# A two-layer gated cross-attention kernel: a loop written out, work of GpSimd put in another order, and extra matmuls on zeros in TensorE's waits

## The reference, cut to what matters

```python
x = x + tanh(g_xattn[0]) * L0_xattn(ctx, layernorm(x))   # context and latents as keys, 4 heads of 64
x = x + tanh(g_ffn[0])   * L0_ffn(layernorm(x))          # 256 -> 1024 -> 1024 -> 256, weights of +1 and -1
x = x + tanh(g_xattn[1]) * L1_xattn(layernorm(x), ctx)   # 16 heads of 64, 1024 keys
x = x + tanh(g_ffn[1])   * L1_ffn(layernorm(x))          # 16 experts, 4 of them per token, and one shared

# L0_xattn: q and k are RMS-normed per head; the keys are 1024 of the context (masked) and 512 latents
attn = softmax(where(mask, qn @ kn.T, -max)); out = (attn @ v) @ Wo.T + bo
# L1_xattn
out = softmax(q @ k.T / 8) @ v @ Wo + bo
# L1_ffn
y = sum_e combine[:, e] * (silu(x @ w1[e].T) * (x @ w3[e].T)) @ w2[e].T + shared expert
```

## Time and profile before

| | us |
|---|---|
| median of three runs | 1186.76 |
| lowest and highest | 1183.84, 1190.51 |
| the profiled execution, its own time | 1189.64 |
| its span (first to last instruction) | 1187.8 |
| PE busy | 1082.3 (91%) |
| DVE busy | 837.9 (71%) |
| ACT busy | 700.5 (59%) |
| POOL busy | 354.9 (30%) |
| mean granted TensorE clock | 0.971 of full |

### The profile page before, as it was taken

One profiled execution on the slowest core, in us unless ns is written; L12 is line 12 of the kernel. 1 busy time (PEld: TensorE's weight loads), 2 busy tenths in 40 slices (PEclk: granted clock), 3 DMA queues, 4 the chain that ended last, 5 costly groups with the idle time before them and its releaser, 6 DMA issues. The chain is left out here.

```text
span 1187.8 us, 20470 instructions
## 1 busy us (share of the span) xinstructions
PE 1082.3 (91%) x6952; PEld 947.2 (80%) x6952; DVE 837.9 (71%) x1437; ACT 700.5 (59%) x1273; POOL 354.9 (30%) x372
## 2 busy tenths in 40 slices
PE   1879988998899899999989999999999879999998
PEld 1768877787787778888879798888888768888887
DVE  7687756777514498888879788788889565555555
ACT  3477756775623487787867777787877412222232
POOL 5064415442377402101040203111020213344341
PEclk9899998999999999999999999999999879999999
DMA  4000000002022000000100010000000005343432
GB/s 137 21 1 1 1 5 1 1 1 88 25 57 55 26 1 2 1 1 1 37 3 1 1 37 2 2 1 1 28 1 1 27 5 144 93 124 101 115 109 68
DMA packets 20344, 39.47 MB, mean 33 GB/s; under 512 B 5056, under 2 KB 12352, under 8 KB 19744
## 3 DMA queue, kind: packets, MB, share of 16 engines
q1 hardware_dynamic: 20256, 38.32, 10.9%
HBM read 37.07 MB, written 1.25 MB: 32 GB/s over the span
## 5 line engine op out<-in xcount | busy, mean ns | idle before, releaser
L281 PE MATMUL PS<-R 128*128 128x512 f32 (+2 forms) x2728 | 627.7, 375 | 47.5 <-issue 14.7
L281 PEld LDWEIGHTS PS<-R 128*128 128x128 f32 x2728 | 461.6, 196 | 124.6 <-issue 26.9
L1389 DVE TENSOR_TENSOR R<-PS,R 128x512 fp32r<-128x512 f32 x320 | 205.5, 683 | 37.2 <-ACT R L1107 36.3
L1107 ACT ACTIVATE R<-PS 128x512 fp32r<-128x512 f32 x320 | 175.5, 595 | 83.3 <-PE PS L648 82.6
L1073 ACT ACTIVATE FA<-PS,nmax 128x1024 f32<-128x1024 f32 (+1 forms) x160 | 192.4, 1203 | 41.8 <-DVE nmax L1378 21.8
L661 PE MATMUL PS<-R 128*128 128x256 f32 x1408 | 203.1, 290 | 10.4 <-DVE FB L1397 9.1
L648 PEld LDWEIGHTS PS<-eye,FA 128*128 128x128 f32 x1408 | 163.2, 142 | 43.8 <-DVE R L1389 11.0
L648 PE MATMUL PS<-eye,FA 128*128 128x128 f32 x1408 | 189.5, 279 | 8.9 <-ACT FA L1073 3.5
L661 PEld LDWEIGHTS PS<-R 128*128 128x128 f32 x1408 | 179.1, 190 | 18.3 <-issue 14.5
L1378 DVE TENSOR_REDUCE nmax<-PS 128x1 f32<-128x1024 f32 x128 | 155.8, 1221 | 40.8 <-PE PS L281 29.6
L436 POOL TENSOR_SCALAR R<-R 64x512 fp32r<-64x512 f32 x40 | 25.9, 649 | 327.2 <-ACT R L1222 266.7
(11 more groups left out here) (173 smaller groups left out, 1071.3 us busy)
## 6 DMA issues: line engine op xcount, KB each, us to landing
FB<-comb SPq DMA_DIRECT2D x48, 256.0 KB, 3.8
wst<-we_in SPq DMA_DIRECT2D x26, 384.0 KB, 4.0
wst<-w_in SPq DMA_DIRECT2D x4, 1024.0 KB, 5.0
FB<-k_in SPq DMA_DIRECT2D x16, 128.0 KB, 2.0
wst<-w_in SPq DMA_DIRECT2D x3, 512.0 KB, 5.8
x<-x_in SPq DMA_DIRECT2D x2, 512.0 KB, 5.6
FB<-ctxT_in SPq DMA_DIRECT2D x2, 512.0 KB, 4.7
FB<-ctxT_in SPq DMA_DIRECT2D x4, 256.0 KB, 3.8
```

Of the source, the lines that this page charges most:

```text
L281: last = mm(out, a, b, start=(n == 0), stop=(n == len(passes) - 1), skip_group_check=skip)
L1107: a_(L.pt[0][:, (u // 2) % 2, 4 * g_:4 * g_ + 4, (u % 2) * P:(u % 2) * P + P], L.turn(u, g_).rearrange("p (t n) -> p t n", t=4), ACT.Copy) ...
L1389: inc(v.tensor_tensor(lo, turned, hi.bitcast(F32), ALU.subtract), "p_lo")
```

## The change

1. **Loop.** The `Fori` over the second attention's three turns becomes a Python `for` on PE, ACT, DVE and POOL: the same instructions, once for each turn, with constant counts.
2. **First attention, low halves in order of need.** POOL copies slots 0 and 1 of the queries, makes the low halves 0 to 4, then copies slots 2 and 3, then makes the low halves 5 to 7. PE awaits two copies ahead of the first scores, and all four ahead of unit 8.
3. **First exponential.** ACT awaits three low halves of each engine ahead of the first exponential, and all eight ahead of its first `third` copy.
4. **Zeroing in waits.** The two memsets of `zero_spare_queries(L0, 2)` move ahead of line 474's copy in batch 1, behind a wait for the two output projections of batch 0 (`wo_done` 2).
5. **Matmuls on zeros.** Ten ahead of the feed-forward part's first block (behind a wait for `zeroed`); at the head of the expert stage the two that stood ahead of `gate_up(0)` become eight behind it and eight behind `ln_turn`, and ten are added ahead of `down(1)`. Their results are overwritten or add nothing.

```diff
-        def copy_queries(L, C, count):
+        def copy_queries(L, C, count, slots=range(HG)):
...
-            for slot in range(HG):
+            for slot in slots:
...
             last.then_inc(s["bo_added"], 1)
+            if b == 1:
+                pool.wait_ge(s["bo_added"], 2)
+                pool.wait_ge(s["wo_done"], 2)
+                zero_spare_queries(L0, 2)
 
             pool.wait_ge(s["cx_hi"], 4 * b + 4)
...
-            copy_queries(L0, b, (8 * b + 2, 8 * b + 2))
-            if b == 1:
-                zero_spare_queries(L0, 2)
+            copy_queries(L0, b, (8 * b + 2, 8 * b + 2), range(2))
 
             for i in range(8):
+                if i == 5:
+                    copy_queries(L0, b, (8 * b + 2, 8 * b + 2), range(2, HG))
                 pool.wait_ge(s["qk0_hi"], 8 * b + i + 1)
...
-        with pool.Fori(1, NG1) as i:
+        for i in range(1, NG1):
...
-                pe.wait_ge(s["q_twice"], HG * C + HG)
+                pe.wait_ge(s["q_twice"], HG * C + 2)
...
                 if L.layer == 0 and u + 2 == UNITS // 2:
+                    pe.wait_ge(s["q_twice"], HG * C + HG)
...
+            if j == 0:
+                pe.wait_ge(s["zeroed"], 1)
+                for n in range(5):
+                    for w in range(2):
+                        mm(PS[:, 4 + w, :], zero, LNH[:, 0, 512:1024], start=True, stop=False, skip_group_check=True)
             if m == 0:
                 pe.wait_ge(s["ln_lo"], 2 * NB + 2 * (h + 1))
...
-        with pe.Fori(0, NG1 - 1) as i:
+        for i in range(NG1 - 1):
...
-        zero_banks(4)
-        zero_banks(5)
         gate_up(0, 0, 0, 0)
+        for n in range(4):
+            zero_banks(4)
+            zero_banks(5)
         pe.wait_ge(s["x_att"], 4 + 4 * NG1)
         ln_turn(4 * NB + 2, LN_BANKS[1], late1)
+        for n in range(4):
+            zero_banks(4)
+            zero_banks(5)
         down(0, 0, 0, 0)
...
         gate_up(2, 1, 1, 0)
+        for n in range(5):
+            zero_banks(6)
+            zero_banks(7)
         down(1, 0, 0, 1)
...
                         if g_ == 2:
+                            if u == 0:
+                                act.wait_ge(s["qk0_lo"], 8 * C + 8)
+                                act.wait_ge(s["qk0_lo_pool"], 8 * C + 8)
                             first(act, "p_third", U0 + u - 1)
...
-            act.wait_ge(s["qk0_lo"], 8 * b + 8)
-            act.wait_ge(s["qk0_lo_pool"], 8 * b + 8)
+            act.wait_ge(s["qk0_lo"], 8 * b + 3)
+            act.wait_ge(s["qk0_lo_pool"], 8 * b + 3)
...
-        with act.Fori(0, NG1 - 1) as i:
+        for i in range(NG1 - 1):
...
-        with dve.Fori(0, NG1 - 1) as i:
+        for i in range(NG1 - 1):
```

## The result

| | before | changed |
|---|---|---|
| median of 5 runs, us | 1190.51 | 1176.74 |
| lowest and highest | 1183.84, 1192.71 | 1174.45, 1180.80 |
| the profiled execution: its time, its span | 1189.64, 1187.8 | 1178.63, 1176.5 |

What follows compares the result with a forecast made beforehand. PE, busy 91% of the span, was taken to bound the kernel through idle and lower-clock stretches. Terms summed to -11.15 us: 1178.5 from the profiled 1189.64, 1175.6 from the median 1186.76; forecast 1176, 8-in-10 range 1170 to 1183.

Steps and rivals of the forecast that it cites:

- Loop, -6.3: Second attention: writing the loop out removes two jumps costing 3.28 and 2.99 us; bounds -5 to -7.
- hidden already: Second attention's loop: the register arithmetic for the counts also goes, but was given no gain.
- Batch 0, -1.6: First attention, batch 0: two copies fewer ahead bring the first exponential 1.6 us sooner; bounds 0 to -2.4.
- Batch 1, -3.5: First attention, batch 1: two copies and two memsets fewer ahead bring the exponential 3.5 us sooner; bounds -1.5 to -3.6.
- The +0.7 for a lower clock: First attention, batch 1: lower clock over the transposes after longer PE idle time costs 0.7 us, middle of 0 and 1.5.
- Memsets, +0.65: Gap between batches: memsets delay line 474's copy, and PE with it, by 0.65 us; bounds 0 to +1.
- Zeros ahead of the feed-forward part, +2.6: Feed-forward start: ten matmuls on zeros push the layer norm's root and transposes back, costing 2.6 us; bounds 0 to +5.3.
- Nothing later absorbs it: After the feed-forward zeros: the delay carries on, since the next stage waits for the last of these blocks.
- Head, -3.7: Expert stage's head: zeros fill PE's gaps, keeping full clock over down(0) and the router; saves 3.7 us, bounds -5.3 to +5.8.
- the larger value: Expert head: -5.3 us if gate_up(1) and (2) also run at full clock; not taken.

Runs made afterwards that it cites:

- e1: The kernel before with only the second attention's loop written out on four engines; ratio to before 0.9957, 1185.08 us.
- e10: The changed kernel with PE's loop over the expert tiles written out too; ratio to before 0.9906, 1178.60 us.
- e5: The kernel before with only the low halves in order of need, PE awaiting two copies; ratio to before 1.0000.
- e6: The kernel before with only the first exponential's wait cut to three low halves of each engine; ratio to before 1.0000.
- e6b: The kernel before with the order of need and the shorter exponential wait together, nothing else; ratio to before 0.9982.
- e8: The changed kernel with the feed-forward zeros moved behind block 3 and the two memsets behind line 474's copy; ratio to before 0.9875, 1175.01 us.
- e11: The changed kernel with nine wide matmuls on zeros mixed between the router's groups; ratio to before 0.9909, 1178.67 us.
- e2: The changed kernel without the ten matmuls on zeros ahead of the feed-forward part; ratio to before 0.9883, 1177.45 us.
- e3: The changed kernel with the expert stage's head as before, two matmuls on zeros ahead of gate_up(0); ratio to before 0.9931, 1183.23 us.
- e7: The changed kernel with the ten feed-forward zeros moved from ahead of block 0 to behind block 3; ratio to before 0.9892, 1173.84 us.
- e4: The changed kernel with the two memsets back behind the copies of query slots 0 and 1; ratio to before 0.9924, 1180.84 us.
- e8b: The changed kernel without the feed-forward zeros and with the two memsets behind line 474's copy; ratio to before 0.9894, 1175.46 us.

## Why the prediction was right

The forecast was 1176 with a gain of 11.15 us from the profiled execution; measured were 1176.74 and, between the two profiled executions, 11.0. By its steps:

1. **Loop, -6.3**: the mechanism is as predicted (no wait on issue in the turns, e1, e10). The term was 0.9 too small. The six blocks of the three turns take 388.7 us in place of 395.9, 7.2 less, which is 3.45 and 3.15 for the two with a jump and about 0.16 for each of the other four. The step gave the register arithmetic nothing, "hidden already"; it is the only part of the edit that touches the blocks without a jump. One reading was wrong: the second q8 packet of the first jump starts at 611.3 us, behind PE's idle stretch (608.07 to 610.78) and not in it. The first starts with the stretch, at 608.0, and takes 1.2 us, so the fetch covers under half of the 2.71 us, and what the rest is stays open.
2. **Batch 0, -1.6**: 1.2 between PE's free moment and the exponential, the same in all ten traces with edits 2 and 3 (5.4 to 5.5 us in place of 6.7). The step let PE wait 70.5 - 70.15 = 0.35 us for the fifth low half; it waits 0.68, so two copies fewer bring that half 2.35 - 0.68 = 1.67 us closer, not 2.0, and the exponential follows 0.4 later than said. That neither edit works alone is shown by e5 and e6.
3. **Batch 1, -3.5**: 3.7 between these two traces. In the seven others with the memsets out of the way the exponential follows PE's free moment by 5.5 us, not 4.85, and by 8.1 in e1 and e6, not 8.54, so 2.6 to 3.0 is nearer. The +0.7 for a lower clock behind the longer idle time was put in the wrong batch: batch 1's transposes ran at full clock (1.50 us), while in batch 0 a stretch of 6.8 us at half clock begins at 78.2, in e6b, e8, e10 and e11 as well, while e2, e3 and e7 have half of it, as the kernel before, and e4 and e8b none. So the lower clock may follow the longer idle time, in the other batch and not in each execution; chance is not excluded.
4. **Memsets, +0.65**: +0.6, shown by PE's idle time of 3.86 against 3.27. What the move wins in batch 1 stands under step 3.
5. **Zeros ahead of the feed-forward part, +2.6**: the path (root, apply, transposes) moved by 2.9 as derived, the 2.79 us of idle time did not cover it. "Nothing later absorbs it" holds where the clock is the same, 3.3 and 2.0 us at the start of the second attention. The times don't show it: e2's, 0.9883 against 0.9898, is 1.8 us less, with room for 0 as for 2.6.
6. **Head, -3.7**: 14.50 us in place of 18.63 from `down(0)` to `down(1)`, 4.1, and 3.9 by the times of e3. The half clock behind the router, on account of which the larger value was not taken, came in this execution and in four of the six others with this head and router, but not in e4 and e7; that the narrow matmuls bring it is not shown, also not by e11.

That the sum came out so close is partly luck. The errors cancel: step 1 gave 0.9 more, step 2 gave 0.4 less, and the clock differs between any two executions by more than what is left. And 1176 was counted from the first median, 1186.76; from 1190.51, the median of five, the same sum gives 1179.4, while the measured gain is then 13.8 us by the medians, 12.1 by the ratio.

A jump of the experts' loop costs nothing that can be seen (e10), a jump of the second attention cost 3.28 and 2.99 us. The Trainium skill's figure for a branch ("Advanced Engine Details and Errata", Control Flow Timing, about 108 ns) is too small by a factor of about thirty for the second; the first does not show it, its turns take 16.71 to 16.73 us with the jump and without.

In the changed kernel PE is busy for all of the 16 us from 938 to 954, and the granted clock falls all the same, to the lower level at 945.2. "TensorE: Matmul & The Clock Gate", Part 1, of the Trainium skill goes by how busy the PE has recently been, and by that alone the clock would stay up there; it would also not stay down over the earlier trace rows. Both speak against busy time alone, as the prediction said, and neither says what else counts.

## What to carry to other kernels

A hardware loop was free here where its jump fetches nothing, and cost PE's path about 3 us at each jump of the long body; the place to look is a wait on "issue" with an instruction fetch beside it. Filling a wait with work on zeros can keep TensorE's clock up, as at the head of the experts. It is free only where the fill does not push back what another engine needs for the next step: find the first thing that is queued behind the filled place on *other* engines. And two waits in series want to be taken away together; each alone measured nothing here. Where the clock moves by itself, compare traces with the same time at half clock in the stage; a trace that has the wanted clock already ahead of the edit proves nothing for it.

## What the runs showed of the hardware that was not expected

- TensorE can be at the lower clock while the profile shows it fully busy. Over 24 matmuls of 16 columns PE is busy for 5.00 of 5.00 us at a granted 0.50; in the changed kernel the same 24 run at 1.00, and the clock falls 1.1 us behind them with no idle time of PE in between. In e4 and e7 it does not fall there, so narrow matmuls are a suspect and no more.
- The counts of a hardware loop seem to cost something even where no engine waits on "issue": blocks without a jump take 64.92 to 64.95 us in the four kernels with the loop and 64.76 to 64.80 in the ten without.
- Two executions that differ in one place get another clock in places that are the same in both. e7 has full clock from 213 to 919 us; e2, which is e7 without the ten zeros, drops to the lower level at 296, 375 and 409 us, the last two behind code that is the same in both. e5 and e6 differ in the same way, over stages that neither touches. One stretch of 3.4 us near the end of the second attention costs 1.4 us there (42.9 us in nine kernels that have it, 41.5 in five that don't). The clock moves a stage by 1 to 3 us, which is as much as most edits of this change are worth, and what sets it was not settled.
